# One call for all four feature strips, and a new order of work on four engines, in a two-layer gated cross-attention kernel

## The reference, cut to what matters

```python
# layer 0, attention: random features, causal, no softmax
q = q * 128**-0.25; k = k * 128**-0.25                  # 16 heads of 8
q_prime = exp(q @ R) + eps                              # R: 8 x 32 features
k_prime = exp(k @ R - 0.5*|k|^2 - max(-0.5*|k|^2)) + eps
out = causal(q_prime @ k_prime.T) @ v / the same with ones for v
x = x + tanh(g) * out
# layer 0, feed-forward
out = sigmoid(xr @ Wr.T) * (square(relu(xk @ Wk.T)) @ Wv.T)
# layer 1, attention: a softmax, and a softmax of the gated softmax
attn  = softmax(q @ k.T * scale)
attn2 = softmax(gate * attn)                            # gate = mean and max over the context
out   = (w * attn2 + (1 - w) * attn) @ v
# layer 1, feed-forward: gated, 512 wide, with rounded activations and weights
```

## Time and profile before

| what | us |
|---|---|
| median of 2 executions | 497.62 (496.18 to 499.07) |
| the profiled execution | 501.52 |
| its span, first to last instruction | 499.8 |
| time around the span | 1.72 |
| mean granted TensorE clock | 0.960 |

### The profile page before, as it was taken

One profiled execution on the slowest core, in us unless ns is written; L12 is line 12 of the kernel. 1 busy time (PEld: TensorE's weight loads), 2 busy tenths in 40 slices (PEclk: granted clock), 3 DMA queues, 4 the chain that ended last, 5 costly groups with the idle time before them and its releaser, 6 DMA issues.

```text
span 499.8 us, 19032 instructions
## 1 busy us (share of the span) xinstructions
PE 459.6 (92%) x7622; PEld 339.1 (68%) x7622; DVE 414.4 (83%) x1369; ACT 367.6 (74%) x774; POOL 302.2 (60%) x416
## 2 busy tenths in 40 slices
PE   6589899999999999999999999999999999797864
PEld 3266677777778686868687777777786868475532
DVE  5752695989999998989898989899998989977834
ACT  5436676878797969797978788787979696855642
POOL 6421365776767675858585757667676757472720
PEclk9956999999999999999999999999999999958997
DMA  7401010101010010101010101010110100000000
GB/s 228 112 3 27 21 38 10 42 5 52 4 31 26 16 43 12 47 10 47 9 51 8 50 7 50 5 40 17 22 35 12 46 12 14 10 15 1 12 12 10
DMA packets 31526, 15.15 MB, mean 30 GB/s; under 512 B 12496, under 2 KB 30800, under 8 KB 31440
## 3 DMA queue, kind: packets, MB, share of 16 engines
q1 hardware_dynamic: 31296, 13.92, 10.6%
q10 hardware_dynamic: 144, 0.02, 0.0%
HBM read 9.73 MB, written 2.10 MB: 24 GB/s over the span
## 4 chain that ended last, share of the span: by engine, by line
PE 63%; DVE 20%; issue 5%; DMA 4%; ACT 3%; SPq 2%; POOL 1%; DVEq 0%
PE MC L1558 13%; PE TP L1523 9%; PE FP L1434 6%; PE MA L1450 6%; DVE SL L1047 4%; PE SP L1626 3%; PE SP L1514 3%; DVE emn L1053 3%; DMA Cd<-in_ctx 2%; PE FP L1413 2%; PE SP L1498 2%; PE FP L1370 2%; PE FP L1373 2%; PE MA L1479 2%; PE FP L1417 1%
## 5 line engine op out<-in xcount | busy, mean ns | idle before, releaser
L1558 PEld LDWEIGHTS MC<-Vc,ET 128*64 128x64 f32 x2048 | 66.7, 141 | 22.9 <-issue 20.1
L1558 PE MATMUL MC<-Vc,ET 128*64 128x25 f32 x2048 | 73.4, 221 | 1.4 <-DVE X L1161 0.8
L411 POOL TENSOR_SCALAR ft<-ft 128x512 f32<-128x512 f32 x64 | 39.5, 617 | 52.0 <-ACT ft L637 48.3
L434 POOL TENSOR_TENSOR Zn<-E,rsh 128x1024 f32<-128x1024 f32 x32 | 60.9, 1902 | 10.8 <-DVE rsh L1061 9.4
L442 POOL TENSOR_TENSOR Zn<-Zn,Gs 128x1024 f32<-128x1024 f32 x32 | 60.9, 1902 | 1.2 <-DVE Gs L1071 1.1
L684 ACT ACTIVATE ET<-TP 128x512 f32<-128x512 f32 x64 | 36.6, 598 | 31.8 <-PE TP L1523 31.8
L1001 DVE TENSOR_TENSOR WT<-FP,mask 128x512 f32<-128x512 f32 x64 | 41.9, 676 | 8.2 <-PE FP L1434 8.2
L1434 PE MATMUL FP<-ft 32*64 32x64 f32 x2048 | 38.5, 225 | 8.0 <-DVE WT L1001 5.4
L1434 PEld LDWEIGHTS FP<-ft 32*64 32x64 f32 x2048 | 34.1, 137 | 14.3 <-issue 5.2
L1041 DVE TENSOR_REDUCE mx<-SP 128x16 f32<-128x1024 f32 x32 | 39.0, 1218 | 3.6 <-PE SP L1514 3.4
L678 ACT ACTIVATE ET<-TP 128x512 f32<-128x512 f32 x64 | 37.6, 587 | 4.9 <-PE TP L1523 3.8
(11 more groups left out here) (210 smaller groups left out, 1180.5 us busy)
## 6 DMA issues: line engine op xcount, KB each, us to landing
Cd<-in_ctx SPq DMA_DIRECT2D x32, 128.0 KB, 3.0
kX<-kT SPq DMA_DIRECT2D x256, 8.0 KB
X<-in_x SPq DMA_DIRECT2D x16, 128.0 KB, 2.7
call<-in_ctx SPq DMA_DIRECT2D x4, 512.0 KB, 5.5
out_x<-X SPq DMA_DIRECT2D x16, 128.0 KB, 2.1
wffn<-in_L_ffn_w_gate SPq DMA_DIRECT2D x1, 256.0 KB, 5.4
wffn<-in_L_ffn_w_up SPq DMA_DIRECT2D x1, 256.0 KB, 5.7
wffn<-in_L_ffn_w_down SPq DMA_DIRECT2D x1, 256.0 KB, 6.7
```

Of the source, the lines that this page charges most:

```text
L411: pool.tensor_scalar(f, f, EPS_K, 1.0, ALU.add, ALU.mult).then_inc(s("ftp"), 1)
L434: pool.tensor_tensor(z, E1[u][:, :].rearrange("p (h m) -> p h m", m=64), rsh[u][:, :].unsqueeze(2).to_broadcast([P, H, 64]), ALU.subtract) ...
L1558: last = mm(MC[64 * j:64 * j + 64, c + 32 * q:c + 32 * q + 25], weights[:, q, 64 * j:64 * j + 64], Vc[g.p][:, 2 * u + j, q, 0:25], start=T ...
```

## The change

Features of all four strips come from one call: strips 0 and 1 go to the two banks of `FP`, strips 2 and 3 to the two banks of `SP_`. So the call also waits until VectorE has read the scores of stage c out of `SP_`. ScalarE then takes four exponentials in a row, GpSimd its four additions in a row.

```diff
-            def features(g, w):
+            def features(g):
 
                 at_ends(pe, g, s("WT"), g.k * 4)
...
+                at(pe, s("Vc"), g.k * 2)
+                at(pe, s("csq"), g.k + 1)
+                at(pe, s("kT"), g.k)
+                at(pe, s("qcT"), g.k + 1)
+                at(pe, s("ls"), g.k * 2 - 2)
+                strips = [(32 * i, (FP, SP_)[i // 2], 512 * (i % 2), i) for i in range(4)]
+                for r, bank, o, i in strips:
                     mm(bank[:, o:o + 256], Rf[r:r + 32, i, :], qcT[r:r + 32, 0:256], start=True, stop=True)
...
             def features(g, w):
 
-                at(act, s("f"), g.k * 2 + 1 + w)
-                f = (SP_ if g.first and w == 1 else FP)[:, :].rearrange("p (i t n) -> p t i n", i=2, t=2)
+                if w == 0:
+                    at(act, s("f"), g.k + 1)
+                f = (FP, SP_)[w][:, :].rearrange("p (i t n) -> p t i n", i=2, t=2)
...
                     if a.first:
                         constants()
                         clear_values()
+                        clear_keys()
                     ftp(a, 0)
...
-                v.scalar_tensor_tensor(rsh[u][:, :], emn[u][:, :], 1.0, pos[g.p][:, u, :], ALU.mult, ALU.max).then_inc(s("rsh"), 1)
+                v.tensor_tensor(rsh[u][:, :], emn[u][:, :], pos[g.p][:, u, :], ALU.max).then_inc(s("rsh"), 1)
...
-                v.scalar_tensor_tensor(Gs[u][:, :], gate[g.p][:, u, :], 1.0, rs1[u][:, :], ALU.mult, ALU.mult).then_inc(s("Gs"), 1)
+                v.tensor_tensor(Gs[u][:, :], gate[g.p][:, u, :], rs1[u][:, :], ALU.mult).then_inc(s("Gs"), 1)
```

More of the change, by code:

```diff
@@ L775, in step @@
                     if b.first:
-                        round_weights()
-                    yB(b)
+                        wait_setup()
+                    shift_rows(b)
+                if e:
+                    ffn_mid(e, 1)
+                if c:
+                    softmax1n(c, 1)
                 if a:
@@ L1193, in step @@
                     causal(b, 2)
+                if c:
+                    mvC(c)
+                if b:
                     causal(b, 3)
+                if e:
+                    ffn_h(e, 0)
+                if c:
+                    gates_mean(c)
+                if e:
+                    ffn_hu(e, 0)
+                if d:
+                    gated(d, 1)
+                if e:
+                    ffn_hmax(e, 0)
+                if d:
+                    gated_G(d, 1)
+                    first(d, 1)
+                if e:
+                    ffn_hscale(e, 0)
+                    ffn_hrec(e, 0)
+                if c:
+                    nbC(c)
                 if a:
@@ L1655, in step @@
             def step(a, b, c, d, e):
-                if c:
-                    if c.first:
-                        warm(1)
-                    ffn0_out(c)
                 if d:
@@ L1707, in step @@
                 if d:
-                    turn2(d, 3)
-                if a:
-                    if a.k == 1:
-                        warm(2)
-                    rows_T(a)
+                    turn2(d, 2)
+                if b:
+                    if b.first:
+                        warm(4)
+                    gates_sum(b)
                 if c:
                     queries(c)
+                if d:
+                    turn2(d, 3)
+                if c:
+                    scores(c, 0)
                 if d:
@@ L1718, in step @@
                     outB(d, 1)
-                if b:
-                    gates_bc(b)
+                if a:
+                    if a.k == 1:
+                        warm(3)
+                    rows_T(a)
                 if c:
-                    scores(c, 0)
+                    gates_bc(c)
+                if e:
+                    if e.k == NG - 2:
+                        warm_end(1)
+                    if e.k == NG - 1:
+                        warm_end(9)
+                    ffn_down(e, 0)
+                if c:
+                    scores(c, 1)
                 if d:
@@ L1726, in step @@
                     project_T(d)
+                if b:
+                    if b.first:
+                        wait_setup()
+                        warm(2)
+                    rows_BT(b)
+                if d:
+                    if d.k == NG - 1:
+                        warm_end(1)
+                    project(d)
+                if e:
+                    if e.k == NG - 3:
+                        warm_end(2)
+                    if e.k == NG - 1:
+                        warm_end(1)
+                    ffn_down(e, 1)
                 if a:
@@ L1731, in step @@
                     if a.k == 1:
-                        warm(2)
-                    features(a, 0)
-                    if a.first:
-                        warm(4)
-                    gates_sum(a)
-                if d:
-                    if d.k == NG - 1:
-                        warm_end(1)
-                    project(d)
+                        warm(3)
+                    features(a)
+                if c:
+                    turn1(c, 0)
+                    turn1(c, 1)
                 if e:
@@ L1744, in step @@
                     if e.k == NG - 1:
-                        warm_end(8)
-                    ffn_down(e, 0)
-                if b:
-                    if b.first:
-                        wait_setup()
-                        warm(2)
-                    rows_BT(b)
-                if a:
-                    features(a, 1)
-                if c:
-                    scores(c, 1)
-                    turn1(c, 0)
+                        warm_end(1)
+                    ffn_dn(e, 0)
                 if b:
@@ L1781, in step @@
                     if a.k == 1:
+                        warm(2)
+                    weights0(a, 0)
+                if b:
+                    if b.first:
                         warm(1)
-                    weights0(a, 0)
+                    ffn0_out(b)
             run(pe, step)
```

332 lines of the change are left out of this document (141 added, 191 removed).

## The result

The changed kernel takes 512.78 us (median of 2 executions, 510.80 and 514.77) against 497.62: 1.029 times the time before, 95% interval 1.019 to 1.040. The forecast was 500.6, range 490 to 510. It is slower, and by more than the range held. (Ratios and intervals here leave out executions more than 1.5% above the fastest of their kernel; medians and ranges are over all.) The profiled execution is the one of 514.77, with a span of 513.0; that of before has 499.8. So 13.2 us are to be found, where the forecast had 3.0.

What follows compares the result with a forecast made beforehand. The prediction took TensorE to bound the kernel before and a ring of waits the changed one. Start -0.5, full steps +6.7 and end -3.2 gave +3.0 us: 504.5 profiled, 500.6 against the median, range 490 to 510.

Steps and rivals of the forecast that it cites:

- What bounds the kernel now: Full steps before the change: TensorE bounds them, busy 26.20 of 26.48 us, with some 0.3 us of holes.
- The features on TensorE: Four strips run four wide in 1.61 us, 1.5 us less TensorE work a step, a floor of 24.7.
- The wait that it adds, the ring: Full steps: waiting for SP_ closes a ring through all engines of 27.12 us, 0.56 longer a step, +6.7 us.
- The other edits of a full step: Simpler VectorE operation, swapped order, earlier key transfers and work moved over the step boundary: taken as zero.
- The start: Filling steps up to step 4: early clearing and full clock against a longer ring in steps 2 and 3, -0.5 us.
- 3 us of this are gone: Case within the start: if the clock falls despite the early clearing, 3 us of the gain are lost.
- The end: Steps 16 to 18: +0.5, -2.5 and -1.2, sum -3.2 us; near zero with the clock low as before.
- The sum: Whole kernel: -0.5 + 6.7 - 3.2 = +3.0 us, 504.5 on the profiled 501.52, 500.6 against the median.
- TensorE stays the bound: Rival: full steps fall with TensorE's work to about 25.1 us, 476 us in all; chance 0.08.
- The edges give more: Rival: full clock throughout and steps 2 and 3 shorter than the ring, 492 us; chance 0.18.
- ScalarE takes the ring over: Rival: ScalarE's list delays project(d) and the exponentials; 0.7 us of delay gives steps of 27.8, 509 us; chance 0.18.
- Two pairs: Rival: the four strips run as two pairs, +1.5 us a step in 14 steps, 521 us; chance 0.04.

Runs made afterwards that it cites:

- experiment 6: Row maximum over 4 of 64 columns, keys cleared in step 0, otherwise the kernel before: one features call in the old order 500.87 us, two calls 490.03.
- experiment 3: Changed kernel with row maximum over 4 of 64 columns, 505.17 us; with ScalarE's attended-rows copy ahead of stage c's first exponential, 511.16; with both, 494.82.
- experiment 4: Changed kernel with proj_ctx(b) moved behind outB(d,1), 529.74 us; also with the attended-rows copy moved earlier and additional unused matmuls in steps 0 to 2, 524.97.
- experiment 1: Changed kernel with 52 additional unused matmuls in the idle stretches of steps 0 to 2: 510.61 us, 1.025 times before.
- experiment 5: Changed kernel with features in two calls, 559.72 us; kernel before with early clearing and one features call, 509.77; the latter with 11 more unused matmuls, 512.58.
- experiment 2: Kernel before with only the clearing of both key buffers moved from step 1 to step 0: 493.77 us, 0.987 times before.

## Why the prediction was wrong, by its steps

**What bounds the kernel now**: right. TensorE does: 2 us less of VectorE's work moved the step by less than 0.1 us (experiment 6).

**The features on TensorE**: right. Four wide, 1.63 us for 1.61, and the floor that came from it, 24.7, is the 24.72 of the window.

**The wait that it adds, the ring**: right in its sum (27.06 for 27.12) and in each piece, the largest error being the 0.10 us of outA to scores. Its account of what holds the step was half of it. "ScalarE ends only some 0.1 us before the features want it" named the second chain, with its distance, and experiment 3 measured 0.1. The prediction made of it a rival that would decide by its delay; it is no rival but a second wall, and with the VectorE ring 2 us shorter the step is still 26.95 us. The ring's piece on TensorE, outA to scores, was taken as plain order, and experiment 4 found a chain right behind that too.

**The other edits of a full step**: right at zero. The form with one operation less is held beside GpSimd like the old one: it takes 0.65 us in the row below, where a product of 1.91 us runs on GpSimd, and 0.18 in the median of its 32 uses.

```profile
458.83 0.65 DVE L1069 TENSOR_TENSOR Gs<-gate,rs 128x16 f32<-128x16 f32 x1
...
457.55 1.91 POOL L434 TENSOR_TENSOR Zn<-E,rsh 128x1024 f32<-128x1024 f32 x1
```

By the rule of the Trainium skill (SBUF — State Buffer, SBUF: two separate sides) that the prediction weighed, it is held because of its two SBUF inputs, whatever the operation, against a GpSimd instruction that reads SBUF; the trace agrees, as it ends 0.02 us after the product.

**The start**: this is the step that failed. Its working was right at full clock (94.44 in experiment 1 for 94.4), its assumption about the clock was not. The prediction had the full clock return with the early clearing and put "3 us of this are gone" on the other case. What it left out is that the ring, which it had just worked out for step 2, also makes holes in the filling steps, where the work of stages d and e isn't yet there to fill them: 1.64 us at the end of step 1, with the clock at half from 52.8, and then 0.92 and 2.10 us in step 2, with TensorE busy 4.2 of 6 us from 60 to 66. So the half clock did not stay behind in step 1, it went through step 2 and stretched the ring's own pieces from 3.80 to 4.70 us. With matmuls put into the holes of steps 0 to 2 the clock was full and the 7.6 us were gone (experiment 1); which hole brought the fall at 52.8 stays open. 3.0 us were lost in step 1 and 4.4 in step 2. The range had no case for that; the worst clock in it was 3 us.

**The end**: the right sign, mis-sized: -1.1 for -3.2. Step 16 took 25.40 (25.1), step 17 23.84 (22.8), outA to outB(d,1) 10.35 us (9.3), the last stretch 25.4 (25.7). The clock has a small part in it: in experiment 1 step 17 is at 1.00 throughout and takes 23.52 (447.60 to 471.12), 0.3 less. Two pieces were taken too short: outA to scores in step 17, 11.21 us (453.37 to 464.58) and 10.89 at full clock for 10.3, and the 9.3, which assumed that the second exponential, already taken, was what had set the 10.5 before.

**The sum**: 504.5 was forecast for a profiled execution; 514.77 was measured. 7.6 of the difference is the clock at the start, 2.1 the end, 0.5 steps. Against the median the miss is 12.2 us. The prediction took off 3.9 for the median, since the profiled execution of before was that much slower than the others; after, the median lies only 2.0 below the profiled execution, whose mean clock was 0.957 for 0.975 in the other. Where the other lost its clock is not on record.

**The rivals.** "TensorE stays the bound" fell: TensorE has 2.3 us of holes. "The edges give more" was the opposite of what happened. "ScalarE takes the ring over" gave 509 us, nearest in number, for a reason that did not occur: `project(d)` through `attended(d)` is in the chain, but taking 0.48 us out of it moved the step by 0.02 (experiment 3). "Two pairs" fell.

What stays open: why some full steps of the changed kernel and of experiment 1 are 0.3 to 1.2 us longer than their neighbours, at full clock and with waits that the profile gives to no other instruction (in experiments 4 and 5 many of the long steps hold a stretch at half clock instead); and what of the start's time an execution loses to the clock from one run to the next, since it isn't in the program.

## What to carry to other kernels

A call that packs more into TensorE must be priced by what empties its banks. Here 1.5 us of TensorE time a step were freed, and with the old order and with the new one the step came out longer than before (by 1.0 and 0.6 us): the borrowed banks tied two stages together that had been independent, and ScalarE got its exponentials in one block. A call and the order made for it are also to be measured apart: within the new order the call gave 1.8 us, while the order itself had cost 2.35. Once a kernel is balanced to some tenths, two or three chains end together, and an experiment that relieves one says nothing until another is relieved with it. And a wait added in a steady loop is also added in the steps that fill the pipeline, where nothing covers it: price the clock there as well. When two kernels are compared, compare steps at the same granted clock first: here one stretch of 3.4 us at half clock made 30.5 us of a step of 28.83.

## What the runs showed of the hardware

- Four strips of 32 rows into four banks: twelve matmuls, 1.63 us to the reader; six in two banks took 1.61.
- Clearing by GpSimd held a VectorE instruction of 128 x 2 elements for the whole 3.57 us; moved ahead, the same instruction took 0.16. With that line alone moved the kernel took 0.987 times as long (experiment 2, 0.979 to 0.995).
- One stretch of 3.4 us at a granted 0.50 in a step of experiment 5 made it 1.7 us longer (30.5 for 28.83), though it was the same code; TensorE was busy for the whole of the stretch, behind two holes (0.83 us ahead of `project`, 1.37 ahead of the second call).
- The mean granted clock of one kernel, the one before, lay between 0.950 and 0.986 in 22 executions, and its time between 502.59 and 489.96 us.
- With eleven more matmuls the clock stayed at 1.00 over a stretch of 32 us, and was 0.57 over the next 8 us. More activity in one place gave no assurance for the place behind it.
